# State-stationary update gate, z turned on the vector engine, and another order inside a recurrent step

## The reference, cut to what matters

```
# first layer, x: its input, h starts at 0
z = sigmoid(x_t @ W_z + h @ U_z + vz)        # update gate
r = sigmoid(x_t @ W_r + h @ U_r + vr)        # reset gate
c = tanh(x_t @ W + (r * h) @ U + vh)         # candidate
h = (1 - z) * h + z * c
x1_t = x_t + h
# second layer, h1 starts at cond, leak = 1 - alpha (one number per feature)
g  = sigmoid(h1 @ Wh.T + x1_t @ Wz.T + b)
h1 = tanh(h1 * leak + g * x1_t)
x2_t = x1_t + h1
```

## Time and profile before

| what | number |
|---|---|
| median of 3 runs | 983.35 us |
| profiled execution | 983.02 us, span 981.2 us |
| busy share of the span | PE 96%, PEld 78%, DVE 82%, ACT 66%, POOL 22% |
| mean granted PE clock | 0.98 of full speed |
| DMA | 42.01 MB, mean 43 GB/s |

### The profile page before, as it was taken

The page is one execution under the profiler, slowest core; times in us unless marked ns, Lnnn a source line. Parts: engine busy times, 40 slices in busy tenths (PEclk is TensorE's granted clock), DMA queues, the critical chain, the costliest instruction groups (busy, mean ns, idle before and its releaser), DMA issues.

```text
span 981.2 us, 112517 instructions
## 1 busy us (share of the span) xinstructions
PE 938.0 (96%) x50966; PEld 762.4 (78%) x50966; DVE 802.8 (82%) x2373; ACT 644.8 (66%) x2863; POOL 220.1 (22%) x430
## 2 busy tenths in 40 slices
PE   6799999999999999999999999959999999999996
PEld 6699999999999999999999998335555555555554
DVE  2478788888888777877887887799999999999993
ACT  3478777777777777777777776325555555545552
POOL 0011111111111111111111111324434334433340
PEclk7799999999999999999999999979999999999999
DMA  5022321330100100101001001100001000001001
GB/s 178 11 78 80 110 97 50 122 110 28 35 27 24 37 24 26 36 24 37 24 27 35 27 24 33 28 1 25 24 28 44 24 24 24 24 24 47 26 24 43
DMA packets 38294, 42.01 MB, mean 43 GB/s; under 512 B 5120, under 2 KB 31232, under 8 KB 37120
## 3 DMA queue, kind: packets, MB, share of 16 engines
q1 hardware_dynamic: 37120, 41.08, 13.0%
q10 hardware_dynamic: 1152, 0.66, 0.2%
HBM read 32.80 MB, written 8.91 MB: 43 GB/s over the span
## 4 chain that ended last, share of the span: by engine, by line
PE 55%; DVE 31%; issue 8%; ACT 3%; DMA 1%; ACTq 1%; DVEq 0%
PE bank L789 30%; PE bank L735 22%; DVE arena L668 11%; DVE early L687 4%; DVE early L678 4%; ACT cand_kept L393 2%; DVE early L691 2%; DVE early L666 2%; DVE early L672 2%; DVE early L685 2%; DVE none_h L605 2%; DMA bias<-in_bias 1%; PE bank L924 1%; PE bank L878 1%; DVE h_pre L631 1%
## 5 line engine op out<-in xcount | busy, mean ns | idle before, releaser
L735 PE MATMUL bank<-x_ahead,early 128*32 128x64 f32 x12376 | 344.2, 223 | 4.5 <-issue 2.6
L735 PEld LDWEIGHTS bank<-x_ahead,early 128*32 128x32 f32 x12376 | 238.8, 110 | 2.0 <-issue 2.0
L789 PE MATMUL bank<-none_h,early 128*32 128x32 f32 x16384 | 203.2, 199 | 6.4 <-issue 2.9
L282 POOL TENSOR_TENSOR x<-x_f,h_gx 128x64 f32 x256 | 87.5, 342 | 523.2 <-PE bank L789 522.1
L789 PEld LDWEIGHTS bank<-none_h,early 128*32 128x32 f32 x16384 | 180.5, 110 | 24.8 <-DVE none_h L605 13.1
L907 PE MATMUL bank<-x,wl 128*128 (+1 forms) x384 | 181.7, 612 | 0.9 <-DVE rank_rows L647 0.9
L789 PE MATMUL bank<-rh_f,early 128*32 128x32 f32 x8192 | 151.7, 199 | 5.0 <-issue 2.3
L907 PEld LDWEIGHTS bank<-x,wl 128*128 128x128 f32 x384 | 68.9, 191 | 88.6 <-issue 88.6
L789 PEld LDWEIGHTS bank<-rh_f,early 128*32 128x32 f32 x8192 | 122.9, 112 | 7.0 <-DVE rh_f L593 4.6
L605 DVE TENSOR_TENSOR_SCAN none_h<-zero_z,cand_kept 128x64 f32<-128x64 f32 x512 | 121.3, 278 | 5.6 <-ACT cand_kept L393 4.1
L789 PE MATMUL bank<-h_gx,early 128*32 128x32 f32 x8288 | 121.3, 199 | 0.7 <-ACT h_gx L404 0.7
(11 more groups left out here) (98 smaller groups left out, 1289.7 us busy)
## 6 DMA issues: line engine op xcount, KB each, us to landing
x_in<-in_x SPq DMA_DIRECT2D x34, 256.0 KB, 2.7
x_ahead<-in_x SPq DMA_DIRECT2D x130, 64.0 KB, 1.8
arena<-in_w SPq DMA_DIRECT2D x8, 1024.0 KB, 6.0
out<-y SPq DMA_DIRECT2D x32, 256.0 KB, 2.4
rank_rows<-in_bias_rows SPq DMA_DIRECT2D x1, 1024.0 KB, 6.7
arena<-scratch SPq DMA_DIRECT2D x64, 16.0 KB
early<-in_cx SPq DMA_DIRECT2D x1, 768.0 KB, 4.7
early<-in_wx SPq DMA_DIRECT2D x1, 768.0 KB, 6.4
```

The costliest lines, as they stand in the source:

```text
L282: pool.tensor_tensor(x2[:, :, :, s], x1_f[:, u % LOOP], h1_gx[:, u % 2, :, :, 0], ALU.add).then_inc(x2_done, 1)
L735: mm = pe.matmul(out[32 * j:32 * j + 32], weights(k, j, m), moving(k), start=False, stop=False, tile_position=(0, 32 * j), skip_group_chec ...
L789: mm = pe.matmul(out[32 * j:32 * j + 32], weights(k, j, m), moving(k), start=False, stop=k == 1, tile_position=(0, 32 * j), skip_group_che ...
```

## The change

1. The products of the update gate swap their operands: the state (or the input) becomes the stationary operand (32 batch columns) and the weights the moving one, 64 columns (`by_rows`). 8 matmuls a step with 64 columns take the place of 16 with 32. Their result, `pre_z`, has batch on partitions. The input products and the constant part of z are made in the same layout; the input products of z are made for one step at a time (2 x 8 matmuls of 64 columns in the place of 16 of 64).
2. ACT makes z once, into `z_rows`; `keep_f` is gone. DVE turns it with a 32 x 32 block transpose into `zero_z` (L607), and makes `(z - 1) * h` from that (L612). The candidate's tanh takes `scale=-1`, and the scan subtracts its second operand.
3. DVE's `x1` of a step moves into the next step, between the transpose and `(z-1)*h`. gate*x1 and the leaky sum come after both state scans.
4. ACT's tanh of the second layer moves from the end of a step to behind the next step's z, and the second gate's sigmoid from before the candidate to behind it.
5. PE: the second gate's products and the input products of x1 come after the candidate's; no other matmul stands between the candidate's quarters; 32 records of input products stand between the gates and the candidate in each step.
6. The leaky sum of the second layer is two `scalar_tensor_tensor` (one for each half), with the leak as a number for each partition, in the place of a scan over pairs.
7. Semaphores: `reset_seeded`, `x1_ready`, `turned` are new; SP waits on `kept_done` for its loads of `x_in`; SP's last turn is written out.

```diff
-            def gates_first(n, u):
+            def reset(n, u):
                 t, par, v = n * BODY + u, (u // STEPS) % 2, u % STEPS
                 for m in range(HALVES):
                     act.wait_ge(r_pre, 2 * t + m + 1)
                     act.activation(r_f[:, m], pre_rh[par][m][:, 0, v, :], ACT.Sigmoid).then_inc(r_done, 1)
+
+            def update(n, u):
+                t, par, v = n * BODY + u, (u // STEPS) % 2, u % STEPS
                 act.wait_ge(z_pre, t + 1)
-                act.activation(zero_z[:, u % 2, :, :, 1], pre_z[par][:, :, v, :], ACT.Sigmoid).then_inc(z_done, 1)
-                act.activation(keep_f[:], pre_z[par][:, :, v, :], ACT.Sigmoid, scale=-1.0).then_inc(z_done, 1)
+                act.activation(z_rows[:, u % 2], pre_z[par][:, v, :], ACT.Sigmoid).then_inc(z_done, 1)
...
             def turn(n, first=False):
                 for u in range(BODY):
                     second = not first or u >= LAG
-                    gates_first(n, u)
+                    reset(n, u)
+                    update(n, u)
+                    if not first or u > LAG:
+                        second_state(n, u)
+                    elif u:
+                        act.activation(idle[:, u - 1:u], var_eps[:], ACT.Copy).then_inc(h1_done, 1)
+                    candidate(n, u)
                     if second:
                         second_gate(n, u)
-                    candidate(n, u)
...
+            def update_turned(n, u):
+                t = n * BODY + u
+                dve.wait_ge(z_done, t + 1)
+                dve.transpose(zero_z[:, u % 2, :, :, 1], z_rows[:, u % 2]).then_inc(turned, 1)
+
+            def kept_state(n, u):
+                t, now = n * BODY + u, (u + 1) % 2
+                dve.wait_ge(turned, t + 1)
+                dve.scalar_tensor_tensor(cand_kept[:, u % 2, :, :, 1], zero_z[:, u % 2, :, :, 1], 1.0,
+                                         none_h[:, now, :, :, 1], ALU.subtract, ALU.mult).then_inc(kept_done, 2)
...
-                flat = lambda w: w.rearrange("p h b a -> p (h b a)")
-                dve.tensor_tensor_scan(flat(h1_pre[:, at]), flat(zero_leak[:]), flat(h1_gx[:, 1 - at]),
-                                       0.0, ALU.mult, ALU.add).then_inc(pre1_done, 1)
+                for m in range(HALVES):
+                    new = dve.scalar_tensor_tensor(h1_pre[:, at, m], h1_f[:, 1 - at, m], keep1[:, m, 0:1], gx_f[:, m],
+                                                   ALU.mult, ALU.add)
+                new.then_inc(pre1_done, 1)
...
+            def by_rows(out, moving, weights, parts=range(HALVES)):
+
+                for k in parts:
+                    for j in range(SLABS):
+                        mm = pe.matmul(out[32 * j:32 * j + 32], moving(k), weights(k, j), start=False, stop=False,
+                                       tile_position=(0, 32 * j), skip_group_check=True)
+                return mm
...
                 pe.wait_ge(h_done, 1)
                 reset(0, 0)
-                keep(0, 0)
-                keep(0, 1)
+                update(0)
                 pe.wait_ge(h_done, 2)
                 reset(1, 0, taken=h_done).then_inc(r_pre, 1)
                 reset(0, 1)
                 reset(1, 1).then_inc(r_pre, 1)
-                keep(1, 0)
-                mm = keep(1, 1)
-                if late_keep:
-                    mm = late_keep()
-                mm.then_inc(z_pre, 1)
+                update(1).then_inc(z_pre, 1)
...
+            def even(u):
+                par, nxt = u // STEPS, 1 - u // STEPS
+                first_gates(u)
+                pe.wait_ge(ahead_loaded[nxt], 16)
+                pe.wait_ge(reset_seeded, 2)
+                ahead_first(nxt, 0, 0).then_inc(reset_seeded, -2)
+                ahead_first(nxt, 0, 1)
+                first_cand(u)
+                second_gate(u)
+                second_inputs((LOOP - STEPS, 0)[par], nxt)
+
+            def odd(u):
+                nxt = 1 - u // STEPS
+                first_gates(u)
+                ahead_first(nxt, 2, 0)
+                ahead_first(nxt, 2, 1)
+                first_cand(u)
+                second_gate(u)
+                ahead_update(nxt, 0)
+                ahead_update(nxt, 1).then_inc(ahead_loaded[nxt], -16)
```

More of the change, by code:

```diff
@@ L216, in next_turn @@
                                  ).then_inc(ahead_loaded[c % 2], 16)
-                    if c == 6:
+                    if c == 6 and not last:
                         next_steps(n, 0)
@@ L220, in next_turn @@
                         sp.dma_start(dst, src).then_inc(done, 16)
-                next_steps(n, 1)
+                if not last:
+                    next_steps(n, 1)
             next_turn(0)
@@ L227, in _ @@
                 next_turn(w + 2, [(w2[w][:, s], io["w2"][:, w, s], w2_in[w]) for s in range(2)])
-            with sp.Fori(6, TURNS) as n:
+            with sp.Fori(6, TURNS - 1) as n:
                 next_turn(n)
+            next_turn(TURNS - 1, last=True)
             sp.wait_ge(rows_done, 4)
@@ L424, in turn @@
                         seed_gate(((u - LAG) // STEPS) % 2)
-                    if second:
-                        second_state(n, u)
-                    else:
-                        act.activation(idle[:, u:u + 1], var_eps[:], ACT.Copy).then_inc(h1_done, 1)
             turn(0, first=True)
@@ L560, in _ @@
                 seed(seed_rh[:, m, 0], 0, m)
-                seed(seed_rh[:, m, 1], 2, m)
-            for m in range(HALVES):
-                seed(seed_z[:, m], 1, m)
+                seed(seed_rh[:, m, 1], 1, m)
+            for v in range(STEPS):
+                dve.tensor_tensor(seed_z[:, v], pre_const_z, bias_rows[:, 1], ALU.add).then_inc(seeds_ready, 1)
             dve.wait_ge(adapter_in, 16 * len(ADAPTER_LOADS))
@@ L613, in first_output @@
                     dve.wait_ge(x2_done, t - LOOP + 2)
[L614 to L618 removed]
                 dve.tensor_tensor(x1_f[:, u % LOOP], x_in[:, slot, u % SLOT], none_h[:, nxt, :, :, 1],
[L620 removed]
+                                  ALU.add).then_inc(x1_ready, 1)
             def second_gated(n, u):
@@ L637, in turn @@
                     reset_state(n, u)
+                    update_turned(n, u)
+                    if first and u == 0:
+                        dve.memset(idle[:, LAG:LAG + 1], 0.0).then_inc(x1_ready, STEPS)
+                    elif u == 0:
+                        first_output(n - 1, BODY - 1)
+                    else:
+                        first_output(n, u - 1, first)
+                    kept_state(n, u)
+                    next_state(n, u)
                     if second:
                         second_gated(n, u)
-                    next_state(n, u)
-                    if second:
                         second_sum(n, u)
-                    first_output(n, u, first)
             def adapter_rows(w):
@@ L830, in first_cand @@
                 cand(0, 0)
-                hole()
                 pe.wait_ge(rh_done, 2)
```

146 lines of the change are left out of this document (63 added, 83 removed).

## The result

The changed kernel takes 979.05 us (median of 6 runs, 976.95 to 980.27) beside 983.51 for the kernel before on the same chip: a ratio of 0.995, 95% interval 0.9939 to 0.9961. It is faster, as forecast, but by 4.5 us and not by 18.

The account below looks back on a forecast made before the run. Bound: the scan-to-scan chain, r delayed by the second layer's tanh, the candidate by eight input records. 3 x 2.10 + 2.35 = 8.65 for 8.91, 62.5 times: 16 us, plus 1.5 at the loops of 16, together 18: 965 us; range 948 to 986.

Parts of the forecast that it names:

- The scan chain, 2.10: State scan through gates, r, r*h and candidate's tanh to next scan: 2.09, taken as 2.10 us inside PE's loop.
- z's detour, 2.11: z on ACT, transpose, `(z-1)*h`, then the scan: this chain ends at 2.11 us, the same point as the candidate's.
- the rival that it sets the end: z's detour over DVE sets the step's end: with the long transpose 34 us slower, 1017 us; chance 0.14.
- Second PE: candidate from 1.51, 24 records 0.20, second gate 0.27, ... 2.45: PE from candidate to next gates, with 32 input records 0.47: done 0.35 after a scan at 2.10, when the state arrives.
- The return, 0.25 on top: Where PE's loop of four returns, PE begins 0.60 after the scan, not 0.35: that step takes 2.35 us.
- The loops of 16, 1.5 us: At the return of the loops of 16 steps some 0.1 us should go: 15 turns, 1.5 us (0 to 4).
- The first turns, left alone: First turns, outside the stretch of 250 steps, run slower; no gain or loss was forecast there.
- The signs named in advance: Right: scans 2.1 apart, candidate's quarters without filled gap. Wrong: scans over 2.165, transpose's chain last, PE waiting for input products.
- The least likely (0.04, three chains meet): Rival: no change to speak of, three chains meet and their jitter eats the gain, 983 us; chance 0.04.
- A state that is exposed as stationary operand: Rival: PE's state load exposed once or twice (0.11 each) a step: 2.21 and 2.46, 11 us slower, 994; chance 0.05.
- A covered return: Rival: PE done earlier, its loop return hidden: 4 x 2.10, 29 us and 2 at the turns, 952 us; chance 0.17.
- the load at 300.68: PE's load after its loop's return, read as held by the scan: loads already wait for the state, so nothing added.

Follow-up runs that it names:

- e1: Changed kernel with 24 of the 32 input-product records behind the second layer's gate left out in every step; 956.05 us.
- e3: Changed kernel with 8 of the 32 input-product records behind the second gate moved ahead of the candidate; 972.56 us.
- e8: Kernel before, with 24 of the input-product records behind the candidate left out in each step; 978.58 us.
- e2: Changed kernel with the z gate undone (weights stationary, 1-z by a second sigmoid, no transpose), new order kept; 988.85 us.
- e5: Changed kernel with 24 more records of 32 columns in each candidate, behind the wait for r*h's second half; 1031.69 us.
- e4: Changed kernel with TensorE's loop over eight steps in place of four, its body written twice; 1789.71 us.
- e10: Changed kernel with the second gate put back in front of the candidate on TensorE; 1056.50 us.
- e6: e3 with eight more products of zeros in TensorE's set-up, lengthening the code ahead of its loop by 16 pairs; 967.03 us.

## Why the prediction was wrong in size

- **The scan chain, 2.10: right.** e1 and e3 show it wherever TensorE is out of the way. In the changed kernel r begins 0.97 after the scan (0.92 forecast), 0.05 late because the gates begin 0.09 late; the second layer's tanh stands between z and the candidate.
- **z's detour, 2.11: right, and a little dear.** The transpose takes 0.25, kept 0.23; kept ends 1.99 after the scan in e1, as forecast (1.67 + 0.10 + 0.24 = 2.01). Only the last hand-over, 0.10, was too much: from gate times x1 to the leaky sum, both on DVE, it is 0.036 in the trace. By that this chain did not tie but had some 0.07 to spare, and the rival that it sets the end is refuted, by e1 and by the tanh that the scan waits for. VectorE's ten instructions (497.31 of 561.86 us busy, 89%) do not stand against a step of 2.10 either (e1, e3).
- **"Second PE: candidate from 1.51, 24 records 0.20, second gate 0.27, ... 2.45": the step that failed.** The mechanism was there, but the second gate was priced at 8.4 ns a record, where it stood behind a wait. Behind the candidate it takes 303.62 - 303.28 = 0.34. From the gates to the candidate's second half the forecast had 1.51 - 0.35 = 1.16, as measured (304.08 - 2.17 = 301.91 to 303.07, where the candidate's second half begins in the trace); from there to the next gates 0.94, and measured is 304.08 - 303.07 = 1.01. 1.16 + 1.01 = 2.17, the regular step. No run has the second gate at 0.27 behind the candidate; that the round sets the step is shown by e1 and e3, that the gate is what made it too long by this sum. The prediction saw this chain end "just when the next state arrives" and took 2.10 for granted; but two chains that tie leave no room, and 0.07 too little went into the step in full: 3 x 0.07 in four.
- **The return, 0.25 on top: nearly right.** Its price holds (305.80 + 0.66 - 0.22 = 306.24, the last record, to 306.52: 0.28, forecast 0.26), and it is 0.28 in the step, since TensorE is late in every step already: 2.45 and not 2.35. With the above 8.96 - 8.65 = 0.31 in four, times 62.5: 19 us, the 16 that the fours were to give and some more.
- **The loops of 16, 1.5 us: right in the sum, by luck in part.** At the medians of the four steps (8.96) 250 steps make 559.8, and they take 2.1 more; before (8.93) 557.7 and 4.1 more. These 2.0 us make good what the fours lost, 2.1. But not 0.1 of a return went: every sixteenth step was 0.22 over the other returns before and is 2.45 like them now, some 3.5 us. The 2.1 that came back are single steps, two of them (0.43 and 0.60) waits for the DMA of `x_ahead`, which the prediction put at nothing.
- **The first turns, left alone: wrong.** There lies the gain that there is, 4.0 us. The loop's code is 704 pairs where it was 768 (64 records of z a loop less), and the sixth scan moves with the code: 35.5 with 608 pairs (e1), 39.2 with 672 (e8), 38.6 to 40.7 with 704, 41.9 and 43.65 with 768 (e2, before), 42.8 with 800 (e5). The page of the kernel before counts one packet of instructions more than that of the changed one shown above:

```profile
q8 instruction: 12, 0.20, 0.1%
```

It is 12 with 768 and 800 pairs and 11 with fewer. That code is what is loaded there is shown by e4; that it makes up all of the 4.0 is not shown. TensorE's first load of the state comes at 14.68 and not at 16.25, so 1.6 of the 4.0 lie ahead of the loop, and kernels with equally long loops differ by 2 us. The granted clock is not the reason: in the first stretch it is 0.83 in the changed kernel and 0.77 before, but 0.70 in e8, which is as early, though its loop begins at 16.11, as late as before, and only its input products are fewer. First before, then e8:

```profile
0.00:43.65 43.65, 28.48 (x1351) 26.41 (x1355) 14.02 (x69) 16.00 (x69) 2.86 (x10) 0.77 0.30 104
```

```profile
0.00:39.24 39.24, 27.35 (x1222) 25.18 (x1222) 14.12 (x70) 15.97 (x69) 2.86 (x10) 0.70 0.33 116
```

- **The signs named in advance** pointed the right way: scans more than 2.165 apart, and the candidate's tanh as the last thing awaited. That TensorE might no longer wait for the state at all, which tells this case at a glance, was not among them.
- **The rivals.** The least likely (0.04, three chains meet) came nearest: no step was gained, though two chains met and not three, and no jitter was needed. A state that is exposed as stationary operand would have kept e1 and e3 from 2.10. A covered return was mis-added: 8.91 - 8.40 = 0.51 in four is 32 us and not 29. And the load at 300.68 was held by the return, not by the scan at 300.21: PE begins 0.35 after a scan in the other step shown, which is 300.56.

## What to carry to other kernels

When a chain is shortened until it ties with another, add up the other engine's whole round as a loop of its own, with each price taken from a place like the new one (behind a wait or not): a tie is already a bound. Work that fills a wait is not an obstacle by itself; before it is moved behind, ask what stands there. Keep a loop's code small enough that a pass loads none of it, and look at the first records behind its return.

## What was not expected of the hardware

- 32-column records run at 8.4 ns for some 32 records behind a wait, and at 10 to 10.7 on the mean where more follow at once (e10, e5, the changed kernel).
- Twice the loop's code, 1.82 times the time: instruction packets go from 11 to 390, the granted clock of the 250 steps from 1.00 to 0.81 (e4).
- Where the loop's start lies in its code decided over 0.15 us in each return of e3 and e6 (2.50 to 2.57, and 2.385), but the changed kernel, with its loop at the place of e3's, stopped in 1 of 60 returns.
- The two last layers, the same in all kernels, took 374.8 to 380.0 us from kernel to kernel, in one profiled execution of each. What moves them was not looked for; differences of 2 or 3 us in the time are safer read from the steps.
